# Graph-layer score look-ups: masking wrong source tiles by a matmul of -1e30 and a maximum, in place of a multiplication by a one-hot and a sum

## The reference

```python
# layer 1 (8 heads of 32)
alpha = einsum('ehd,hd->eh', h[src], a_src) + einsum('ehd,hd->eh', h[dst], a_dst)
enc = relu(edge_attr @ edge_W.T + edge_b).reshape(-1, H, D)
alpha = alpha + sum(enc * h[dst], axis=-1)
# layer 2, twice (4 heads of 64)
e = alpha_s[src] + alpha_d[dst]
```

## Time and profile before

| | before |
|---|---|
| median of 3 runs | 4497.1 us (4493.14 to 4499.89) |
| the profiled execution: time / span | 4499.97 us / 4498.1 us |
| TensorE busy | 3116.7 us, 69% |
| VectorE busy | 2755.6 us, 61% |
| GpSimd busy | 2308.4 us, 51% |
| ScalarE busy | 1918.1 us, 43% |
| mean granted clock of TensorE | 0.832 |

### The profile page before, as it was taken

The page is one execution under the profiler, slowest core; times in us unless marked ns, Lnnn a source line. Parts: engine busy times, 40 slices in busy tenths (PEclk is TensorE's granted clock), DMA queues, the critical chain, the costliest instruction groups (busy, mean ns, idle before and its releaser), DMA issues.

```text
span 4498.1 us, 64518 instructions
## 1 busy us (share of the span) xinstructions
PE 3116.7 (69%) x15178; PEld 2165.3 (48%) x15179; DVE 2755.6 (61%) x5281; ACT 1918.1 (43%) x4101; POOL 2308.4 (51%) x2109
## 2 busy tenths in 40 slices
PE   3666566567878567566765765565766479999898
PEld 2544444456666434445763444464444344454544
DVE  5776777667989977554488765688865640210303
ACT  1555555437989655333214543413543440310402
POOL 3778787877777377770254777071777300000000
PEclk6888878789999888776767877766987689999999
DMA  9888888845556433343672334182335323132230
GB/s 287 187 182 177 180 183 176 149 133 146 120 114 153 110 97 106 105 133 144 221 246 61 106 105 132 55 273 82 106 105 161 100 66 99 52 110 90 69 94 29
DMA packets 382578, 589.72 MB, mean 131 GB/s; under 512 B 76827, under 2 KB 256532, under 8 KB 382022
## 3 DMA queue, kind: packets, MB, share of 16 engines
q1 hardware_dynamic: 196854, 311.79, 23.6%
q0 software_dynamic: 133024, 219.83, 22.1%
q10 hardware_dynamic: 52528, 56.23, 3.6%
HBM read 447.67 MB, written 139.96 MB: 131 GB/s over the span
## 4 chain that ended last, share of the span: by engine, by line
PE 28%; issue 23%; POOL 19%; DVE 14%; DMA 10%; ACT 4%; DVEq 1%; SPq 0%; POOLq 0%; ACTq 0%
PE ps L908 14%; POOL shared_sb L589 8%; DMA t_neigh<-resid_sb,idx_b 6%; POOL score_sb L589 4%; POOL resid_sb L589 3%; POOL t_neigh L544 3%; PE ps L992 2%; PE ps L800 2%; DVE shared_sb L1622 2%; DMA accum<-t_drel 2%; PE ps L770 2%; PE ps L721 1%; POOL early_sb L589 1%; DVE score_sb L1599 1%; PE ps L849 1%
## 5 line engine op out<-in xcount | busy, mean ns | idle before, releaser
L544 POOL DMA_INDIRECT t_neigh<-resid_sb,idx_b x416 | 653.0, 1570 | 217.7 <-issue 95.1
L589 POOL DMA_INDIRECT shared_sb<-table,idx_a x568 | 549.9, 968 | 328.2 <-issue 233.3
L908 PE MATMUL ps<-score_sb,shared_sb 128*128 128x512 f16 (+1 forms) x3150 | 640.6, 364 | 24.2 <-DVE shared_sb L1733 24.1
L1116 ACT ACTIVATE onehot<-iota,drel 128x128 f32<-128x128 f32 x1248 | 381.9, 388 | 644.2 <-PE ps L849 642.3
L1708 DVE TENSOR_TENSOR accum<-accum,ps 128x264 f32 (+1 forms) x1248 | 535.7, 429 | 190.9 <-DVE accum L1708 53.5
L849 PE MATMUL ps<-shared_sb,onehot 128*128 128x264 f32 (+1 forms) x1136 | 391.6, 503 | 210.8 <-DVE accum L1708 210.8
L576 POOL TENSOR_SCALAR onehot<-iota,carry_d 98x512 bf16<-98x512 f32 x28 | 43.6, 1565 | 945.7 <-PE ps L925 816.8
L690 PE MATMUL ps<-score_sb,onehot 128*128 x832 | 294.1, 515 | 327.3 <-DVE onehot L1485 327.3
L908 PEld LDWEIGHTS ps<-score_sb,shared_sb 128*128 128x128 bf16 x3150 | 308.5, 98 | 345.2 <-issue 18.3
L589 POOL DMA_INDIRECT score_sb<-table,idx_a x288 | 282.3, 980 | 332.8 <-DMA table<-score_sb 159.1
L566 POOL DMA_INDIRECT t_adj<-counts,early_sb x391 | 389.5, 996 | 122.8 <-issue 121.8
(11 more groups left out here) (319 smaller groups left out, 6389.4 us busy)
## 6 DMA issues: line engine op xcount, KB each, us to landing
score_sb<-t_adj SPq DMA_DIRECT2D x105, 640.0 KB, 3.9
onehot<-t_hot SPq DMA_DIRECT2D x208, 256.0 KB
accum<-t_drel SPq DMA_DIRECT2D x208, 128.0 KB, 4.6
accum<-t_src SPq DMA_DIRECT2D x104, 256.0 KB, 5.0
shared_sb<-t_key SPq DMA_DIRECT2D x104, 256.0 KB, 4.3
t_hot<-shared_sb SPq DMA_DIRECT2D x104, 256.0 KB
t_adj<-accum ACTq DMA_DIRECT2D x25, 896.0 KB, 8.8
shared_sb<-t_adj SPq DMA_DIRECT2D x35, 640.0 KB, 10.7
```

What stands on the lines that cost most here:

```text
L544: pool.indirect_dma_start(t_neigh[u], bass.IndirectOffsetOnAxis(ap=idx_b[:, q * L0H + u:q * L0H + u + 1], axis=0), msg[:, q * L0H + u, :], ...
L589: pool.indirect_dma_start(around[g][at][:, u, 0:w], None, tab, bass.IndirectOffsetOnAxis(ap=idx_a[:, at * HU + u:at * HU + u + 1], axis=0) ...
L908: mm = pe.matmul(ps[:, 2 * (i % 3) + f, 0:w], h_gin[:, t, m, f * P:(f + 1) * P], ring["gin"][:, at % HOLD, c, 0:w], start=(t == 0 and m == ...
L1116: last = act.activation(onehot[:, h % 2 * HU + u, :], iota[:, 0:P], ACT.Abs, bias=drel[:, bass.ds(step + u, 1)], scale=-1.0)
```

## The change

Which tile a source lies in is no longer applied by a multiplication. `lo_compare` makes a one-hot of 32 tile numbers for each of the 4 steps of a quarter (partition 32 j + t is step j, tile t) from a broadcast load of tile numbers, written to memory once as `t_lo`; its product with the constant `not_lo` adds -1e30 to the columns of all wrong tiles and 0 to those of the right one, into the same PSUM bank as the scores. VectorE then takes the maximum over 25. In k = 0 the source product is made from three bfloat16 parts of the table and the bfloat16 one-hot `hot_k`, so that `hot_t` is left for the destination alone, and ScalarE makes `hot_k` first. For k > 0 the destination's parts are reduced by VectorE for all 8 columns; ScalarE's copies are gone, and one addition over all steps joins the two at the end. The buffers of the look-up move into the memory of `peak`; the order of the ring in k = 0 changes, GpSimd may issue 64 gathers before it waits there and need not wait in k > 0.

```diff
-        around = [of_resid + of_shared[1:2] + of_early + of_shared[2:] + of_h + of_shared[0:1]]
+        around = [of_resid + of_shared[1:] + of_early + of_h + of_shared[0:1]]
@@ sync, look-ups
+                def load_lo(i, h):
+                    sp.wait_ge(*count("lo_hot", (2 * (S // UN) + 1) * k + 2 * i + h + 1))
+                    sp.sem_inc(done("sp_go"), 1)
+                    sp.dma_start(lo_w[:, h, :, :], t_lo[bass.ds(i * (UN // QU) + 2 * h, 2), :, :].rearrange("k p e -> p k e")).then_inc(lo_in[h], 16)
+                sp.wait_ge(*count("lo_out", 16 * (SB + 1)))
+                load_lo(0, 0)
+                load_lo(0, 1)
...
                     for q in range(UN // QU):
                         keep(i - 1, q)
                         fetch(i, q)
+                        if q % 2 == 1:
+                            load_lo(i, q // 2)
+                load_lo(S // UN, 0)
@@ gpsimd, gathers
-                    if h == (5 if g == 0 else RS // HU - 1):
+                    if g == 0 and h == 8:
                         looked_up()
@@ tensor, look_up
+                        pe.wait_ge(*count("src_used", n + ahead))
+                        pe.wait_ge(*count("lo_hot", 2 + (2 * (S // UN) + 1) * k + 2 * i + q // 2 + 1))
+                        for b in range(2 if k == 0 else 1):
...
+                            pe.matmul(ps[:, b if k == 0 else q % 2, 0:n_to * NT * H], lo_hot[:, q, :],
+                                      not_lo[:, to, :].unsqueeze(2).to_broadcast([P, n_to, H, NT]), start=True, stop=False)
+                        if k == 0:
+                            pe.wait_ge(*count("hot_k", n + 2))
...
+                            for m in range(3):
+                                mm = pe.matmul(out, hot, src_b8[:, m, :] if k == 0 else src_b[:, m, :, :], start=False,
@@ scalar
+            for b in range(SB):
+                act.dma_start(by_steps[b * SQ:(b + 1) * SQ], lo_rows[:, b, :].unsqueeze(1).to_broadcast([SQ, P // QU, P])).then_inc(done("lo_out"), 16)
+            act.dma_start(by_steps[S:S + UN], lo_rows[0:UN, 0, :].unsqueeze(1).to_broadcast([UN, P // QU, P])).then_inc(done("lo_out"), 16)
...
-                        act.activation(hot_t[:, q % 2, :, :], apart[:, :, :], ACT.Relu, bias=ones[:, 0:1], scale=-1.0).then_inc(done("hot_s"), 1)
+                        act.wait_ge(hot_kept[q % 2], 8 * (4 * i + q - q % 2) + 16)
+                        act.activation(hot_k[:, q % 2, :, :], apart[:, :, :], ACT.Relu, bias=ones[:, 0:1], scale=-1.0).then_inc(done("hot_k"), 1)
+                        act.activation(hot_t[:, q % 2, :], apart[:, 1, :], ACT.Relu, bias=ones[:, 0:1], scale=-1.0).then_inc(done("hot_s"), 1)
...
-            def dst_copies(k):
@@ vector, edge_scores
+                def lo_compare(i, h):
+                    dve.wait_ge(lo_in[h], 16 * ((S // UN + 1 - h) * k + i + 1))
+                    dve.wait_ge(*count("src_mm", 4 * (S // UN) * k + 4 * i + 2 * h))
+                    dve.tensor_scalar(lo_hot[:, 2 * h:2 * h + 2, :], lo_w[:, h, :, :], lane_t[:, :], None, ALU.is_equal).then_inc(done("lo_hot"), 1)
...
+                def of_edges(i, q):
...
+                    dve.tensor_reduce(mix[:, :, 33].rearrange("p (b u) -> p b u", b=2), ps[:, 0:2, 0:2 * NT * H].rearrange("p b (u t) -> p b u t", t=NT),
+                                      AX.X, ALU.max).then_inc(done("src_used"), 1)
...
+                lo_compare(0, 0)
                 with dve.Fori(0, S // UN) as i:
+                    for q in range(UN // QU):
+                        if q % 2 == 0:
+                            lo_compare(i + q // 2, 1 - q // 2)
+                        (of_edges if k == 0 else of_nodes)(i, q)
```

More of the change, by code:

```diff
@@ L789, in look_up @@
+                        mm.then_inc(done("src_mm"), 1)
+                        pe.wait_ge(*count("dst_used", n + ahead))
                         if k == 0:
                             pe.wait_ge(*count("hot_s", n + 1 + UN // QU))
-                        else:
-                            pe.wait_ge(wide_in[q], 32 * (S // UN) + 16 * ((S // UN) * (k - 1) + i + 1))
-                        pe.wait_ge(*count("src_used", n + ahead))
                         for j in range(QU):
-                            out = ps[:, j // 2, (j % 2) * NT * H:(j % 2 + 1) * NT * H] if k == 0 else ps[:, q % 2, j * NT * H:(j + 1) * NT * H]
-                            if k == 0:
-                                mm = pe.matmul(out, hot_t[:, q % 2, 0, j * P:(j + 1) * P], src_ht[:, :, :], start=True, stop=True)
-                                continue
-                            for m in range(3):
-                                mm = pe.matmul(out, hot_b[:, q, 0, j * P:(j + 1) * P], src_b[:, m, :, :], start=(m == 0), stop=(m == 2))
@@ L801, in look_up @@
-                        mm.then_inc(done("src_mm"), 1)
-                        pe.wait_ge(*count("dst_used", n + ahead))
-                        if k > 0:
-                            pe.wait_ge(*count("dst_copied", n - S // QU + 1))
-                        for j in range(QU):
-                            hot = hot_t[:, q % 2, 1, j * P:(j + 1) * P] if k == 0 else hot_b[:, q, 1, j * P:(j + 1) * P]
+                            hot = hot_t[:, q % 2, j * P:(j + 1) * P] if k == 0 else hot_b[:, q, 1, j * P:(j + 1) * P]
@@ L1636, in edge_scores @@
-                    if k > 0:
-                        summed(i, quarters - 1)
-                dve.wait_ge(*count("sc_dv", first + per * (S // UN)))
+                    for q in range(UN // QU):
+                        if q % 2 == 0:
+                            lo_compare(i + q // 2, 1 - q // 2)
+                        (of_edges if k == 0 else of_nodes)(i, q)
+                dve.wait_ge(*count("src_used", 4 * (S // UN) * (k + 1) + 2))
+                dve.wait_ge(*count("dst_used", 4 * (S // UN) * (k + 1) + 2))
```

162 lines of the change are left out of this document (87 added, 75 removed).

## The result

The changed kernel took 4800.19 us (median of 4 runs, 4798.18 to 4810.84), the kernel before, in runs beside it, 4495.12 us (4491.78 to 4499.89). The ratio is 1.0683 with a 95% interval of 1.0664 to 1.0702: slower by 305 us. The forecast was 4760, the range 4610 to 4900.

A forecast was written before the change was run, and what follows sets the result against it. Stages had different limits; in the look-up of k = 0 VectorE came first of three engines near their limit. From 4500 us, +3 (start), +303 (k = 0), -9 (after it), -34 (k = 1, 2), less 2.9, gave 4760; range 4610 to 4900.

The forecast's parts named there:

- The stall: Look-up of k = 0: `load_lo` queued behind `fetch` makes VectorE, TensorE and ScalarE stand every two quarters; +303 us.
- Steps of the cycle: Look-up of k = 0, between two compares: compare and maximum, TensorE's burst, load issue, landing; 13.0 us before clock loss.
- the term: Look-up of k = 0: 51 cycles of 15.7 us plus 8, 809 us in place of 506; +303.
- The clock: Look-up of k = 0: TensorE restarts each burst at half clock after standing, adding 2.7 us a cycle.
- the 15.7 of the row: Look-up of k = 0: us for two quarters when each TensorE burst starts at the low clock.
- rival (b): Look-up of k = 0: the stand is there but the clock stays high, 13.0 us a cycle; 4622 us, chance 0.14.
- the row's 5.5: Look-up of k = 0: us TensorE stays at low clock after a wait, read from one burst before the change.
- The start: Program start: small VectorE instructions and five more `t_lo` stores on ScalarE's queue; +3 us, at most 20 for the stores.
- k = 1 and 2: Look-ups of k = 1 and 2: DMA bytes at 311 GB/s set the length, 140 us for 159; -17 us each.
- After the look-up of k = 0: From look-up end to last gather of k = 0, 480 us in place of 489, the ring being full; -9 us.
- (a): Look-up of k = 0: load arrives ahead of the compare, nobody stands, GpSimd becomes the bound; 4403 us, chance 0.10.
- (c): Look-up of k = 0: tile numbers on time, but `hot_k` waits for the store of quarter n-2; 4633 us, chance 0.08.

The follow-up runs named there:

- run 1: Changed kernel with each k = 0 load of tile numbers one pair of quarters earlier in SyncE's queue: 4576.0 us, ratio to before 1.0167.
- run 3: Changed kernel with k = 0 tile-number loads one pair earlier and `hot_k` stores two quarters earlier in SyncE's queue: 4474.9 us, ratio to before 0.9941.
- run 4: Changed kernel with `t_lo` stored once a step and spread over the lanes by the load's source pattern: 4871.7 us, ratio to before 1.0823.
- run 8: On run 3: ScalarE stores tile numbers once into new table `t_loc`, SyncE copies them out 32-fold during layer 0: 4493.9 us, ratio to before 0.9986.
- run 10: As run 8, but `t_loc` declared behind all other scratch tables: 4457.7 us, ratio to before 0.9920.
- run 5: On run 3: the loads of tile numbers in k = 1 and 2 left out, so scores are wrong: 4455.6 us.
- run 11: On run 3: a 104 KB table, written once and never read, put behind `t_lo`: 4514.4 us, ratio to before 1.0036.
- run 2: Changed kernel with each k = 0 store of `hot_k` two quarters earlier in SyncE's queue, loads unmoved: 4906.6 us, ratio to before 1.0901.
- run 12: The kernel of run 3 measured again, unchanged: 4477.7 us, ratio to before 0.9962.
- run 9: As run 8, with a pair's two quarters side by side so look-up loads have 512-byte pieces: 4511.9 us, ratio to before 1.0027.

## Why the prediction was right, and where it was not

**The stall: right, by its own steps.** The load of `load_lo` behind `fetch` in SyncE's queue makes VectorE, then TensorE and ScalarE stand for every pair of quarters. VectorE waits 5.4 us 50 times (forecast 5 to 7, 51 times), and run 1 takes the wait away by the load's place alone. Steps of the cycle, forecast and measured in the cycle shown: compare and maximum 1.25 and 1.25 (1406.73 to 1407.98); end of encoding to the issue 1.71 and 1.83; landing 2.5 and 2.1; TensorE's burst 7.57 and 2.7 for the clock, 10.27 together, and 9.07 here, 9.8 on the mean (15.05 less the 262 / 50 = 5.24 us that TensorE stood ahead of line 822). So the term came out 34 us too large, spread over the landing (2.0 at the median of 47 loads, for 2.5) and the clock. Single instructions were as said: `hot_t`'s ramp 0.70 us (0.65), the maximum 0.98 (0.98), the last reduction 1.29 (1.28).

**The clock.** The granted clock was 0.80 in the stage, 0.95 in run 1 and 0.97 in run 3, for the same matmuls. The burst shown begins at half speed (0.50 in 1408 to 1410) after 5 us of standing. The Trainium skill (TensorE: Matmul & The Clock Gate, HAM oscillation) says this of loops that wait for a transfer between bursts; the trace agrees, with the 0.50. The stage's sum lies nearer the 15.7 of the row than the 13.0 of rival (b). What was too large is the time at the low clock: by the 0.76 of 1410 to 1412 it lasted until about 1411.0 in this burst, 3.0 us and not the row's 5.5, and cost the 1.5 us by which 9.07 exceeds 7.57. A run that holds the clock up while the stall stays was not tried, so its price of about 2.2 us a cycle (9.8 less 7.57) is worked out from rows and not shown alone.

**The start: wrong by 20 us.** The step that failed is the store of `t_lo` on ScalarE's queue: I took 3 us "since bytes at 311 GB/s are 11 us, and ScalarE had that time free there". The bytes at that rate were not the price: the five stores occupied the queue 24.5 us, in which the DMA engines moved only 148 to 160 GB/s (68 to 92 us) at a share of 0.68 to 0.75. The first scatter moved by 27, beyond the 20 of the upper bound, and 23 remained at the look-up. Runs 4, 8 and 10 put it back to 92 to 94 with the wide stores gone.

**k = 1 and 2: wrong in sign, +9 and +5 (+6.5 without the stretch ahead of it) where -17 each stood.** The step that failed is "I take DMA's, since its share was 0.95 there". A busy share was read as a limit. The bytes were right (261 GB/s x 168 us = 43.8 MB for 43.4), the rate was not: the share was 0.84 and no 311 GB/s came. TensorE's busy time and a stand once in a pass filled the stage already before (110 + 49 of 159 us), most of the stand being the reading of the tile numbers; that line of the waits was in the profile of before, and I read only TensorE's 110 us of 164. A stage without the extra loads is back at its old length (run 5), one with them 9 us longer. The misses of 20 us at the start and 48 in k = 1 and 2 are half cancelled by 34 the other way in k = 0. That is luck, and it is why 4760 came within 40 of 4800; the total is better than its terms.

**After the look-up of k = 0: -9 forecast, -9 measured.**

**The rivals.** (a) was priced at 4403 with the load on time. Run 3 is that case, at 4475. The difference is the start (20 us later at the last adjacency scatter) and k = 1 and 2 (+17 for -34). Its mechanism, GpSimd as the next limit, held. (c), the store of quarter n-2, was really there, but masked: ScalarE stood 154 us for it beside the late load, but TensorE stood for ScalarE's `hot_k` only 8.3 us in all (line 832); and it cost 96 us once the load was on time. I had given it as an alternative to the stall; it was the next wait behind it.

**What no part of the prediction had**: the change moved the tables behind `t_lo`, and a megabyte on SyncE's queue in k = 0 went from 74 to 58 us of engine time. That the place is the reason here too is argued from runs 10 and 11, not shown for this pair, whose mix of pieces differs. By it the changed kernel would have been slower still without the move; how much was only measured without the stall (48 us). Part of the 34 us by which the term of k = 0 came out too large may be this move.

## What to carry to other kernels

A transfer issued from an in-order queue is as late as the last wait ahead of it, whosever wait that is (237 us by run 1, 106 the other way by run 2). So when a load is added to a queue, write down for its place which engine's progress each wait ahead of it stands for, and put it behind the oldest one that its buffers allow. Here two reorderings of one queue turned 7% slower into 0.4 to 0.6% faster (runs 12 and 3).

Before a stage's new length is taken from its busiest resource, add to each engine's busy time the stands that no other engine causes, such as a reading at the head of each pass: the engine whose sum fills the stage is the limit. And when a scratch table is added in device memory, declare it last, or measure its place by itself.

## What the runs showed of the hardware that was not expected

- The place of tables in device memory changes the time of reading them. 104 KB more ahead of `t_hi` and `t_drel` raised the engine time per megabyte from 60 to 62 up to 75 us and the stage from 440 to 443 up to 490 us (runs 3, 10, 11, 12). Which distance or alignment it is was not tried.
- Reading sixteen small numbers into registers of TensorE's sequencer took 1.107 us at the median, and TensorE stood for it once in each pass of the look-up of k = 1 (26 readings), for 45 of 168 us together with the branch and the register instructions around it.
- A store with very many small pieces holds the queue that issues it: four of 3328 pieces of 256 bytes took 18.8 us and the fifth, with 512, 5.7 us, where the next one, of 3.2 MB in large pieces, took 0.7.
- The Trainium skill (DMA: Bandwidth & Descriptors, Specifications) wants at least 512 bytes a piece. For these loads of 64 KB no run shows a gain from it: 165.0 us with 512 bytes, 161.6 with 256, where leaving the loads out gives 155.1. The two kernels differ in layer 0 too, and this is one profile of each.
- Layer 0's scatters took 810 to 825 us (first to last) in kernels that do not differ in it, or only by SyncE's 27 copies (853 in run 9, with 108); 10 us in the start of a stage that follows it decide nothing from a single profile.
